# Reading half of the sub-expert gates from DRAM, each row repeated over 32 partitions

## What is computed

```python
S, R, M, K = (8, 16, 64, 4)          # 8 spaces of rank 16, 64 sub-experts in each, the best 4 are used
H, G = (32, 64)
z = jnp.einsum('nd,sdr->nsr', xf, P)
scores = jnp.einsum('nsr,smr->nsm', z, C)
topv, topi = jax.lax.top_k(scores, K)
w = jax.nn.softmax(topv, axis=-1)
...
h = jax.nn.gelu(jnp.einsum('nsr,nskrh->nskh', z, W1g) + b1g)
yl = jnp.einsum('nskh,nskhr->nskr', h, W2g) + b2g
comb = jnp.einsum('nskr,nsk->nsr', yl, w)
out = jax.nn.gelu(comb.reshape(xf.shape[0], S * R) @ G1 + g1b) @ G2 + g2b
```

## Time and profile before

| | us |
|---|---|
| three timed runs | 2108.4, 2109.84, 2111.88; median 2109.84 |
| span of the profiled execution, first to last instruction | 2092.6 |
| first up product of `sub_experts` | starts at 1308.67 |
| last `second` of `sub_experts` | starts at 1630.64 |
| VectorE's L2382, 512 instructions | 262.8 busy |
| ScalarE's L2352, 256 instructions | 227.2 busy |

### The profile page before, as it was taken

How to read it: one execution, slowest core, us unless ns; L and a number is a source line. 1 busy time by engine, 2 the same in 40 slices (tenths; PEclk the granted TensorE clock), 3 DMA queues, 4 the chain that set the end, 5 groups by cost and what they waited for, 6 DMA issues and landing times. The chain is left out here.

```text
span 2092.6 us, 38743 instructions
## 1 busy us (share of the span) xinstructions
PE 1823.8 (87%) x13908; PEld 1324.8 (63%) x14000; DVE 1217.6 (58%) x3641; ACT 837.4 (40%) x1667; POOL 379.2 (18%) x380
## 2 busy tenths in 40 slices
PE   4989969987886799888898875999999999979997
PEld 3678759966674699677665542333333688647886
DVE  1478842237998322378635554788888567891221
ACT  1145413324552111145435554677667355311111
POOL 1100112133312232331001111000000000223543
PEclk8999969998996899889999877999999999999999
DMA  5000245520003455102000115900000000304663
GB/s 202 1 1 0 108 131 178 187 74 18 14 0 141 142 186 182 38 19 87 0 1 17 38 49 145 292 2 1 1 1 1 24 1 0 134 22 124 197 173 65
DMA packets 83838, 156.75 MB, mean 75 GB/s; under 512 B 22389, under 2 KB 57941, under 8 KB 82805
## 3 DMA queue, kind: packets, MB, share of 16 engines
q1 hardware_dynamic: 63669, 134.71, 19.7%
q0 software_dynamic: 19552, 19.63, 3.9%
q10 hardware_dynamic: 480, 0.63, 0.1%
HBM read 125.04 MB, written 29.48 MB: 74 GB/s over the span
## 5 line engine op out<-in xcount | busy, mean ns | idle before, releaser
L2382 DVE TENSOR_TENSOR l2s_gated<-l2s_hidden,ps 128x408 f32<-128x408 f32 x512 | 262.8, 574 | 58.3 <-PE ps L2285 58.0
L2352 ACT ACTIVATE l2s_hidden<-ps,pack_l2f 128x816 f32<-128x816 f32 x256 | 227.2, 938 | 98.1 <-PE ps L2277 97.4
L129 PE MATMUL ps<-pack_const 128*128 128x512 bf16 x496 | 149.7, 437 | 42.2 <-PEq L163 15.3
L2285 PE MATMUL ps<-l2s_gs,l2s_spread 96*128 96x408 bf16 x512 | 150.8, 341 | 0.3 <-DVE l2s_gated L2382 0.3
L2277 PE MATMUL ps<-l2s_zs,l2s_up 128*128 128x408 bf16 x512 | 133.0, 342 | 14.5 <-DMA l2s_gs<-g_parts 14.5
L1895 PE MATMUL ps<-l_down,l_hidden 128*128 x792 | 139.8, 326 | 0.0
L1895 PEld LDWEIGHTS ps<-l_down,l_hidden 128*128 128x128 f32 x792 | 127.3, 190 | 0.4
L129 PEld LDWEIGHTS ps<-pack_const 128*128 128x128 bf16 x588 | 59.7, 109 | 102.1 <-issue 64.6
L2297 PE MATMUL ps<-l2s_gated,l2s_down 128*32 128x408 f32 x1024 | 114.3, 518 | 4.0 <-DVE l2s_comb L2369 3.7
L2277 PEld LDWEIGHTS ps<-l2s_zs,l2s_up 128*128 128x128 bf16 x512 | 39.8, 97 | 119.5 <-ACT l2s_hidden L2352 82.2
L1854 POOL DMA_INDIRECT l_xt<-rows_in,l_tokens x66 | 63.1, 956 | 255.7 <-PE ps L1867 196.5
(11 more groups left out here) (468 smaller groups left out, 3985.0 us busy)
## 6 DMA issues: line engine op xcount, KB each, us to landing
l_up<-in_l_up SPq DMA_DIRECT2D x66, 576.0 KB, 3.8
l3c_wg<-in_l_gate SPq DMA_DIRECT2D x16, 576.0 KB, 4.9
l3c_wu<-in_l_up SPq DMA_DIRECT2D x16, 576.0 KB, 6.2
l3c_wd<-in_l_down SPq DMA_DIRECT2D x16, 576.0 KB, 3.9
slots_out<-l_y SPq DMA_DIRECT2D x66, 96.0 KB, 2.3
l_down<-in_l_down SPq DMA_DIRECT2D x8, 675.0 KB, 9.2
g_parts<-l2b_g_parts SPq DMA_DIRECT2D x12, 408.0 KB, 4.4
l_down<-in_l_down SPq DMA_DIRECT2D x8, 576.0 KB, 7.3
```

Of the source, the lines that this page charges most:

```text
L129: pe.matmul(bank, halves[:, 0:128], halves[:, :], start=True, stop=True)
L2285: pe.matmul(gate_bank(n), spread[:, t % 8, :], gs[half][2 * r + odd][:, t // 8, pair, chunk(n % 2), :], start=True, stop=True).then_inc(ga ...
L2352: act.activation(hidden[:, p % kept, :, :], ps[:, 0, 2 * (p % 2):2 * (p % 2) + 2, 0:NG], ACT.Gelu_apprx_tanh, bias=w.at("b1")[:, s * MT + ...
L2382: dve.tensor_tensor(gated[:, n % ring, :], hidden[:, n // 2 % kept, n % 2, :], gate_bank(n), ALU.mult)\
```

## The change

**In `fusion_and_gates`.** Only two of the four pairs of spaces (`gT_split`) are cut into bf16 parts, so L1447, L1606, L1456 and L1159 work on 204 columns instead of 408, and `g_parts` is half as large. `gT` gets two buffers, and SP stores its other two pairs of spaces as float32 in a new DRAM tensor `g_whole`, one more DMA after each four samples.

**In `sub_experts`.** The first pair of each group keeps its two gate matmuls. For the second pair there are none: for each group SP loads 4 rows of `g_whole` of 816 float32 values, each repeated over 32 partitions, into `whole`, a ring of 6 slots of [128, 2, 408]. VectorE then multiplies both chunks of that pair in one instruction of 816 columns, both inputs on chip in SBUF. `hidden` has 4 slots instead of 3, `gated` 8 chunks instead of 10. In SP's queue six of the new loads stand ahead of the first down weights, the seventh behind everything that the first half needs; the parts for the second half stand among the new loads. From the seventh on, load n waits until the products of group n-6 are done.

```diff
+        gT_split = gT_view[:, 0:4:2, :]
...
+                sp.dma_start(g["g_whole"][:, :, there, :], gT[:, c % 2, 1:4:2, :, :]).then_inc(g_stored[c % 2], 16)
...
-                    act.activation(g_parts[:, n // GB % 2, 0, :, n % GB, :], gT_view, ACT.Copy)
-                    if n >= GB and n % GB == 0:
-                        act.wait_ge(b2_ps, 2 * (n // GB))
-                    act.activation(gT[:, :, n % GB, :], gT_view, ACT.Copy).then_inc(gT_ready, 1)
+                    act.activation(g_parts[:, n // GB % 2, 0, :, n % GB, :], gT_split, ACT.Copy)
+                    if n >= 2 * GB and n % GB == 0:
+                        act.wait_ge(b2_ps, 2 * (n // GB - 1))
+                    act.activation(gT[:, n // GB % 2, :, n % GB, :], gT_view, ACT.Copy).then_inc(gT_ready, 1)
...
-    gates, kept, group, ring = 3, 3, 4, 10
+    gates, kept, group, ring, ahead = 3, 4, 4, 8, 6
...
+        whole = m.sb("whole", [128, ahead, 2, NG])
...
+            def whole_gates(n):
+                half, r, odd, t, _ = order[2 * n]
+                row = 64 * odd + 4 * t
+                if n >= ahead:
+                    sp.wait_ge(gated_ready, 3 * (n - ahead + 1))
+                sp.dma_start(whole[:, n % ahead, :, :].rearrange("p c n -> p (c n)"),
+                             g["g_whole"][row:row + 4, r, half * HALF:(half + 1) * HALF, :]
+                             .rearrange("e b l -> e (b l)").unsqueeze(1).broadcast_to([4, 32, HALF * L]))\
+                  .then_inc(whole_loaded[n % ahead], 16)
...
             def gates_spread(n):
-                half, r, odd, t, pair = order[n // 2]
-                if n >= gates:
-                    pe.wait_ge(gated_ready, n - gates + 1)
-                pe.matmul(gate_bank(n), spread[:, t % 8, :], gs[half][2 * r + odd][:, t // 8, pair, chunk(n % 2), :],
-                          start=True, stop=True).then_inc(gate_ps, 1)
+                half, r, odd, t, _ = order[2 * n]
+                for c in range(2):
+                    j = 2 * n + c
+                    if j >= gates:
+                        pe.wait_ge(gated_ready, 3 * ((j - gates) // 2) + (j - gates) % 2 + 1)
+                    pe.matmul(gate_bank(j), spread[:, t % 8, :], gs[half][2 * r + odd][:, t // 8, chunk(c), :],
+                              start=True, stop=True).then_inc(gate_ps, 1)
...
-            for n in range(2 * pairs):
...
-                dve.tensor_tensor(gated[:, n % ring, :], hidden[:, n // 2 % kept, n % 2, :], gate_bank(n), ALU.mult)\
-                   .then_inc(gated_ready, 1)
+            for n in range(groups):
+                dve.wait_ge(hid_ready, 2 * n + 1)
+                for c in range(2):
+                    dve.wait_ge(gate_ps, 2 * n + c + 1)
+                    dve.tensor_tensor(gated[:, (4 * n + c) % ring, :], hidden[:, 2 * n % kept, c, :], gate_bank(2 * n + c),
+                                      ALU.mult).then_inc(gated_ready, 1)
...
+                dve.wait_ge(whole_loaded[n % ahead], 16 * (n // ahead + 1))
+                dve.wait_ge(hid_ready, 2 * n + 2)
+                at = (4 * n + 2) % ring
+                dve.tensor_tensor(gated[:, at:at + 2, :], hidden[:, (2 * n + 1) % kept, :, :], whole[:, n % ahead, :, :],
+                                  ALU.mult).then_inc(gated_ready, 1)
```

More of the change, by code:

```diff
@@ L1261, in bias_products @@
                     row = 64 * (c % 2) + HP * r
-                    last = pe.matmul(gT_bank[row:row + HP], wf.at("b2", RG)[:, 2 * half + r, :], gT[:, 2 * half + r, :, :],
+                    last = pe.matmul(gT_bank[row:row + HP], wf.at("b2", RG)[:, 2 * half + r, :], gT[:, c % 2, 2 * half + r, :, :],
                                      start=True, stop=True)
@@ L2183, in sub_experts @@
     pairs, per_sum_bank = len(order), len(order) // 2
+    groups, in_bank = pairs // 2, pairs // 8
     with ExitStack() as stack:
@@ new lines, in gates_spread @@
+                for c in range(2):
[4 more added lines that the diff above has]
+                              start=True, stop=True).then_inc(gate_ps, 1)
+            def second(n):
+                half, r, odd, t, _ = order[2 * n]
+                if n % in_bank == 0 and n:
+                    pe.wait_ge(comb_ready, n // in_bank)
+                pe.wait_ge(gated_ready, 3 * (n + 1))
+                if not half and t == 0:
+                    pe.wait_ge(down_loaded[2 * r + odd], 16)
+                for pair in range(2):
+                    for c in range(2):
+                        row = HP * (2 * c + pair)
+                        last = pe.matmul(sums[row:row + HP, :], down[2 * r + odd][:, pair, t, :],
+                                         gated[:, (4 * n + 2 * pair + c) % ring, :],
+                                         start=(odd == 0 and t == 0), stop=(odd == 1 and t == MT - 1))
+                if (n + 1) % in_bank == 0:
@@ L2327, in _ @@
                     up_products(p + 1)
-                for n in (2 * p, 2 * p + 1):
-                    gates_spread(n)
-                if p >= 3 and p % 2 == 1:
-                    second(2 * p - 6)
-            second(2 * pairs - group)
+                if p % 2 == 0:
+                    gates_spread(p // 2)
+                elif p >= 3:
+                    second(p // 2 - 1)
+            second(groups - 1)
             fill(pe, g, ps[:, 0, 2, :], 8)
```

79 lines of the change are left out of this document (37 added, 42 removed).

## The result

The changed kernel takes **2345.12 us** (median of 4 runs, 2343.85 to 2347.02) against 2109.12 us (2108.14 to 2111.88) for the kernel before: ratio 1.1114, 95% interval 1.1095 to 1.1134, 236 us slower. The prediction of 2344 us was right, and so was its cause: the new load is spread over 4 of the 16 DMA engines. That it is right to 1 us is partly luck: two of its terms were mis-sized in opposite directions, and one, the 17 us "around the span", was misread.

A forecast was written before the change was run, and what follows sets the result against it. TensorE and VectorE, near each other, were taken to bound the kernel now, four DMA engines after the change. Span 2092.6 + 236 - 4 + 2 = 2326.6 us, plus 17.2 around it, made 2344 us; range 2300 to 2440.

The forecast's parts named there:

- the 17 us "around the span": Whole kernel: 17.2 us around the span of 2326.6 us, added to make 2344 us.
- The sum: Last `second` of `sub_experts` +236 us, `fusion_and_gates` -4, tail and next layer's start +2; +234 us against the median.
- The period of a group: `sub_experts`: if the data are there, TensorE sets 1.97 us a group, 0.49 less than before.
- Four engines: New load in `sub_experts`: 4 rows against 128 partitions spread over 4 DMA engines, 4.11 us a group; chance 0.80.
- The rate: New load: a packet of 3264 bytes takes 128 ns on one engine, 32 packets an engine, 4.11 us a group.
- The other loads: `sub_experts`: the four engines also move a sixteenth of the stage's other loads, 14.2 MB in all, taken as 40 us.
- The start: `sub_experts`: first down weights stand behind six new loads, 25 us, so the first `second` comes near 1333.
- The waits for `comb`: `sub_experts`: the three waits for `comb` vanish in VectorE's idle time.
- -4: `fusion_and_gates`: VectorE's subtraction loses half its columns and ScalarE's copies shorten; -4 us, bounds -9 and 0.
- The tail, +2: After `sub_experts`: a low clock in the tail and at the next layer's start adds 2 us.
- Sixteen engines: Rival for the new load: spread over all 16 engines, 1.4 us a load, 1.97 us a group, 2070 us; chance 0.10 (sixteen or eight).
- The collision of 32-partition writes: Rival for the new load: four engines collide, 211 ns a packet, 6.7 us a group, 2690 us; chance 0.10.

The follow-up runs named there:

- dimensions 2, 4, 8 and 32: Outer dimension of the changed kernel's new load: two transfers of 2 rows 2841.87 us, 4 unchanged 2345.12, 8 rows 2083.10, repeat outermost (32) 2042.30.
- the kernel without the 122 loads: Changed kernel with only the first six new loads, their slots used again and again (gates wrong from the seventh group on): 2047.12 us.
- the kernel with the repeat outermost: Changed kernel with the new load's source as 32 x 4 x 816 instead of 4 x 32 x 816, second pair's weights reordered to match: 2042.30 us.
- the one-row kernel: Changed kernel with each new load cut into four transfers, one gate row repeated over 32 partitions each: 2124.66 us.
- 128 distinct rows: Changed kernel with each new load taken from 128 different rows, nothing repeated (gates not the right ones): 2042.90 us.
- 8 rows: Changed kernel with each new load of 8 rows repeated 16 times instead of 4 repeated 32 times (other gates): 2083.10 us, one run.

## Why the prediction was right, and where it was not

**The sum.** By stages the change cost 593.2 - 351.4 = 241.8 us in `sub_experts`, where 236 were said, gave 7.3 us in `fusion_and_gates`, where 4 were said, and cost 1.2 us behind, where 2 were said: +235.7 for +234. Two errors of 6 and 3 us cancel in part, and in the first one a larger pair does. That is luck.

**The period of a group.** 1.97 us if the data are there: three kernels show it, and so do the fourth to sixth product after the change. The new product of 1.00 us by slope from the earlier trace rows took 1.008, and 0.92 us from start to start where the next one was ready, as said.

**Four engines.** Right, and shown by dimensions 2, 4, 8 and 32. The reading that carried it came from the trace of before: stores with an outer dimension of 8 at a share of 0.51 and one small packet for each engine.

**The rate.** 128 ns a packet, interpolated between 816 and 4096 bytes; measured 3.95 / 32 = 123 ns, so 20 us less over 128 loads than in the sum.

**The other loads.** 40 us in the sum. The first new load was issued at 1308.20 and the last product started at 1879.6: 571.4 us, less 128 x 3.95 = 505.6, leaves 66 us. In the kernel without the 122 loads, SP's first load of the stage is at 1284.4 and the DMA engines fall idle at about 1364, 80 us; less six loads of 3.95, and less the 3 us that the prediction counts for `pack_l3a`, which there falls inside the 80 us and in the changed kernel comes last, that is 53 us. This term was mis-sized by 13 us at least. Forty us for 14.2 MB are 355 GB/s; the stretch of that kernel in which the other loads run nearly alone shows less, at a share under 1 (columns as in the earlier trace rows):

```profile
1320.00:1364.00 44.00, 39.08 (x266) 12.90 (x266) 35.61 (x55) 32.58 (x37) 0.00 (x0) 0.90 0.88 265
```

Of the remaining 13 us, most are late in the stage: from 1530.34, the 42nd product, to 1879.6 the 86 groups average 4.06. About half of that excess is in five groups of 4.8 to 5 us, the rest mostly in two of every six groups, which take 4.1. With three slots it is one of every three. What makes those longer is open.

The two errors, 20 us too much for the rate and 26 too little for the other loads, nearly cancel: 566 us predicted from first load to last landing, 571 measured.

**The start.** The first `second` was to come at about 1333, on loads that start at 1299; it came at 1347.2 on loads from 1308.2, so 5 us later than said. The waits for `comb` did not vanish: the weight loads of TensorE's `second` waited for it three times, 14.2 us in all. Both sit inside the time of the loads and cost nothing. The run with three slots shows that for the first; for the second, VectorE still waited for its load at every product but the third to sixth, so also right behind each of these waits.

**`fusion_and_gates`.** -4 was taken between 0 and -9; it is -7.3 in this pair of traces. The tail, +2, is +1.2.

**The 17.2 us "around the span".** This step failed. What lies around a span is 1.7 us. The profiled execution of the kernel before was itself about 15 us shorter than that group's median: its stage ahead of `fusion_and_gates`, where nothing was changed, ended at 1041.4, while in the profile after it ended at 1058.4. In all later traces it ended at 1034 to 1045, and the kernel before took 2090 to 2098 us (medians). The two stretches from the first VectorE instruction on `l2a_z` to the start of `fusion_and_gates`, before and after (columns as in the earlier trace rows), hold 16 of these 17 us:

```profile
869.70:1041.40 171.70, 145.42 (x1510) 122.55 (x1527) 125.04 (x386) 82.28 (x159) 41.03 (x46) 0.91 0.11 36
```

```profile
870.80:1058.40 187.60, 151.93 (x1510) 128.49 (x1527) 125.39 (x385) 81.93 (x159) 41.04 (x45) 0.88 0.10 33
```

The same instructions ran, VectorE and ScalarE were busy for the same time, and TensorE's granted clock was lower, 0.88 instead of 0.91. Nothing there was changed, and with three slots the stretch took 171.5 us again, so it is that execution's and not the change's. That the timed runs of the kernel before had the same 16 us fits their times but no trace shows it, and why the clock was lower is open. The total came out right all the same, because the forecast is a difference added to the same group's median.

**The rivals.** "Sixteen engines, 2070 us, 40 less than before" is what the kernel with the repeat outermost does, by 48. The collision of 32-partition writes was real in size: 0.615 x 16 x 20 us / 939 large packets = 210 ns in the one-row kernel, where 211 was said; but with 16 engines it is hidden, and it doesn't touch the four engines.

## What to carry to other kernels

Before a transfer is added to a loop, count the engines it will use, from the outer dimensions of both sides, and divide its packets by that number: a repeat belongs outermost, not inside a short dimension. Then count what issues it: four small transfers in place of one can be bound by SP even with idle DMA engines. Keep no more of them under way than the wait needs: three slots did as well as six. Last, ask which engine a saved instruction belongs to; here the matmuls paid, and the fused VectorE instruction did not.

## What the runs showed of the hardware

- The engines in use ran at 26 GB/s each with 2, 4 or 8 of them (52, 104 and 207 GB/s), 25 if divided by the busy share, as in 104 / (0.256 x 16). With 16 it was less by the same measure: 197 / (0.604 x 16) = 20 GB/s with four rows repeated inside, 155 / (0.615 x 16) = 16 GB/s with 32 partitions at a time.
- SP's time for one issue had a median of 0.32 us (128 distinct rows), 0.51 us (repeat outermost), 0.57 us (8 rows) and 0.59 us (one row of 32 partitions; 0.66 us from start to start in the rows above), but of 3.8 us, up to 8.7, in the changed kernel. The first six new loads wait for nothing in the code, and their six issues took 16.56 us:

```profile
1308.20 16.56 SPq L2259 DMA_DIRECT2D l2s_whole<-g_whole  x6
```

  Slow engines alone do not make the issue long. With three slots the four engines are as far behind, and the issues are short again (ns, minimum, median and maximum; six slots first):

```profile
L2259 SPq DMA_DIRECT2D l2s_whole<-g_whole x128: 506/3829/8747, 1308.2 to 1854.8; - x128
```

```profile
L2259 SPq DMA_DIRECT2D l2s_whole<-g_whole x128: 499/500/4016, 1285.3 to 1845.3; - x128
```

  So the issue of the next transfer gets long when up to six of these loads are under way at once, and not with up to three; where the limit lies, no run shows. While an issue is long, everything behind it in SP's queue is late, also transfers that the twelve idle engines could carry.
